# Diffusion over pairs of tiles, with its first sums kept on chip and the output stage in the same block

## The chip, the cores and the metric

The kernel runs as one program on one core of a Trainium2 chip, all in float32. The metric is the device time of one execution in microseconds (us); lower is better. Three timed runs of the kernel before gave 3935.77, 3936.57 and 3945.05 us, so the median is 3936.57 us. Five engines work side by side, each on its own list of instructions: TensorE (PE: matmuls, with the weight loads as PEld), VectorE (DVE), ScalarE (ACT), GpSimd (POOL, which also issues the indirect transfers) and SyncE (SP, which issues most plain transfers). They wait for each other on semaphores.

## The reference

Four graph layers stand behind each other, each followed by x = layernorm(x + layer(x)). There are 50,000 nodes with 256 features and 12,500 edges, sorted by destination. The first two layers are attention over edges, the third is an edge MLP, and the fourth is the diffusion that the change is about:

```
def _spmm(h, src, dst, inv_deg):
    agg = jax.ops.segment_sum(h[src], dst, num_segments=h.shape[0])
    return agg * inv_deg[:, None]

# layer 3: edge MLP and gate
core = relu(concat(x[src], edge_attr) @ W1 + b1) @ W2 + b2
msg  = sigmoid(concat(x[src], edge_attr) @ Wg + bg) * core
x    = layernorm(layernorm(segment_sum(msg, dst) + x) * gamma + beta + x)

# layer 4: diffusion, six steps
x = silu(h @ W_in.T + b_in)
out = term = x
for i in range(1, 7):
    term = _spmm(term, src, dst, inv_deg) / i
    out = out + term
x = out @ W_out.T + b_out
result = layernorm(h + x)
```

Only nodes that are the destination of an edge get anything from the sums. For all other nodes the four layers are plain row by row arithmetic. The kernel computes all 50,000 rows in that plain way, and afterwards writes the rows of the destination nodes over them.

## The kernel before

**Tables.** The edges lie in T = 100 tiles of 128 slots. For each tile a 128x128 matrix in `eq_tab` says which slots share a destination; a matmul with it sums the messages of each destination. The diffusion works on a table `h` in memory. Its first R = 12,800 rows belong to the tiles; the next R rows (silu of source nodes that are no destination) never change. `table_row` says for each edge which row of the table to gather. A destination can begin in one tile and go on in the next, so after each step the first two rows of every tile are read back (`load_ends`), one matmul with `upper` carries sums across tiles, and the result (`B`, 100 rows) is scattered into the table (`put_bound`). Only then may the next step gather.

**The edge MLP** (`mlp`) runs over 50 pairs of tiles. Its last operation is the silu on ACT into a buffer `HH`, which SP stores to `h`.

**The diffusion** (`diffuse`, L2688) does six steps, by Horner's rule: new row = sum of gathered rows * inv_deg/(6-s) + h. At the start ACT issues ten transfers that bring the 100 tiles of `h` into the on-chip buffer `acc` (L2814) and four that copy the second half of `h` to a second table `h2` (L2818), because the steps read one table and write the other. For every tile and step there is one gather (POOL, L616), one load of the equality matrix (SP, L2726), one matmul (PE, `total`, L2801), one combined multiply and add (DVE, `add`, L2838) and one store (SP, L2731).

**Dense units beside it.** In the same block the class `Dense` computes 160 units of 256 plain rows each. Its instructions are written out in turns: one turn per unit, 165 turns with filling and draining. In a turn PE does four groups, `project` (L810), `transpose` (L674), `out_project` (L828) and `hidden` (L819), and between the groups there are four gaps. `places` (L2676) gives every tile of the diffusion a gap: 110 gaps to a step, a tile in nearly each of the first 100, and the tile-crossing sum five gaps before the end. PE does a tile's sum in its gap, DVE its add one gap later, SP its store two gaps later; POOL gathers eight tiles ahead. POOL also computes all powers of a turn in one instruction (`powers`, L926), for three units in different phases. This power feeds ACT's scales (L851) and DVE's third norm (L900); those feed, one turn later, the variance that the next power needs.

**The output stage** (`output`, L2860 on) is a block of its own behind a barrier. For 50 pairs it loads the sums and `x3`, transposes, multiplies by `w_out`, adds, squares, takes one power per two pairs on POOL (L2894) and writes each tile to `out` by an indirect transfer that POOL issues (L2900).

**What sets the order.** Nothing is scheduled by a tool: each engine follows its own list, written by the loops over turns and gaps, and waits on semaphores. A wait holds up everything behind it on its engine.

## Time and profile before

| what | before |
|---|---|
| median of three timed runs | 3936.57 us |
| span of the profiled execution | 3924.5 us |
| between that span and the median | 12.1 us |
| PE / PEld / DVE / ACT / POOL busy | 83% / 67% / 72% / 48% / 53% |
| edge MLP | about 1800 to 2397 us of the span |
| diffusion block, first instruction to last | 2406.6 to 3723.4 us |
| output block, first instruction to last | 3732.4 to 3914.2 us |

The span runs from the first to the last event of one execution that the profiler recorded. Shares of busy time are means over all stages. What a change does in a stage is read from that stage: which instruction there waits, for what, and whether a later one waits in its turn.

### The profile page before, as it was taken

The numbers are of one execution on the slowest core, as the hardware profiler recorded it, in microseconds if no ns is written. First come the engines' busy times: TensorE is split into PE (matmuls) and PEld (weight loads), VectorE is DVE, ScalarE is ACT, GpSimd is POOL, SyncE is SP. The second block draws the span as 40 slices with busy tenths as digits, with TensorE's granted clock in tenths as the row PEclk, the third lists the DMA queues.
The fourth block names the chain that finished last, engine by engine and source line by source line (L and its number), as shares of the span: only waits on it lengthen the run. The fifth ranks groups of instructions, "written<-read, shape, count | busy, mean of one in ns | idle before, by whom it ended". The sixth has DMA issues, their size and how long they took to land. (4 is left out here: it accounts for less than half of the span.)

```text
span 3924.5 us, 56642 instructions
## 1 busy us (share of the span) xinstructions
PE 3261.1 (83%) x14868; PEld 2626.7 (67%) x14868; DVE 2815.4 (72%) x7890; ACT 1882.4 (48%) x5403; POOL 2087.1 (53%) x2120
## 2 busy tenths in 40 slices
PE   5999927688576899477999993599999999999865
PEld 4888715476454566245777772587878787888754
DVE  5676768698587466794666662598989898989733
ACT  3777705466333121142333331366666666666555
POOL 4767500475365666033333322476767676767667
PEclk8999958899799999657999996799999999999998
DMA  5788739443375333183333335886868686878765
GB/s 145 244 244 247 235 95 354 153 134 108 107 211 174 94 88 87 54 247 99 111 116 115 111 110 187 283 252 199 251 201 252 197 251 201 253 208 242 209 210 164
DMA packets 690467, 710.71 MB, mean 181 GB/s; under 512 B 73444, under 2 KB 644190, under 8 KB 689796
## 3 DMA queue, kind: packets, MB, share of 16 engines
q1 hardware_dynamic: 592204, 484.13, 39.8%
q0 software_dynamic: 68288, 181.26, 17.1%
q10 hardware_dynamic: 29660, 41.70, 3.2%
q8 instruction: 126, 2.06, 0.2%
q14 instruction: 189, 1.55, 0.1%
HBM read 427.77 MB, written 296.22 MB: 184 GB/s over the span
## 5 line engine op out<-in xcount | busy, mean ns | idle before, releaser
L616 POOL DMA_INDIRECT s_i_messages<-h,table_row x600 | 614.0, 1023 | 190.4 <-issue 158.3
L2801 PE MATMUL s_i_bank<-s_i_messages,s_i_equal 128*128 128x256 f32 x1200 | 362.5, 386 | 74.3 <-issue 36.6
L926 POOL TENSOR_TENSOR n_powers<-n_powers,neg_half 128x8 f32<-128x8 f32 (+3 forms) x164 | 268.5, 1637 | 229.9 <-DVE n_powers L891 149.4
L851 ACT ACTIVATE n_z<-gamma_bc,n_powers 128x256 f32<-128x256 f32 x320 | 174.8, 593 | 356.5 <-POOL n_powers L926 356.5
L810 PE MATMUL s_n_bank<-w,n_xt 128*128 128x256 f32 x1280 | 306.9, 383 | 22.6 <-DMA n_xt<-in_x_t 22.6
L828 PE MATMUL s_n_bank<-w_out,n_ht 128*128 128x256 f32 x1280 | 311.7, 387 | 5.6 <-ACT n_ht L838 5.3
L2838 DVE SCALAR_TENSOR_TENSOR s_i_y<-s_i_bank,s_i_scale,s_i_acc 128x256 f32<-128x256 f32 x600 | 285.2, 476 | 34.3 <-PE s_i_bank L2801 32.2
L819 PE MATMUL s_n_bank<-n_x3t,w_in 128*128 128x256 f32 x1280 | 303.2, 380 | 0.0
L2801 PEld LDWEIGHTS s_i_bank<-s_i_messages,s_i_equal 128*128 128x128 f32 x1200 | 219.3, 193 | 101.1 <-issue 42.2
L810 PEld LDWEIGHTS s_n_bank<-w,n_xt 128*128 128x128 f32 x1280 | 246.0, 192 | 58.0 <-DMA n_xt<-in_x_t 23.8
L828 PEld LDWEIGHTS s_n_bank<-w_out,n_ht 128*128 128x128 f32 x1280 | 247.3, 195 | 46.2 <-ACT n_ht L838 11.9
L819 PEld LDWEIGHTS s_n_bank<-n_x3t,w_in 128*128 128x128 f32 x1280 | 243.9, 191 | 33.4
L616 POOL DMA_INDIRECT s_a_x<-in_x,index x200 | 197.8, 989 | 97.4 <-issue 96.3
L2101 PE MATMUL s_e_ps_qv<-w_qv,s_e_xt 128*128 128x512 f32 x400 | 189.7, 597 | 0.0
L2116 ACT ACTIVATE s_e_xt<-s_e_ps_t 128x512 f32<-128x512 f32 x100 | 59.7, 597 | 264.3 <-PE s_e_ps_t L2091 264.3
L2405 POOL TENSOR_TENSOR s_g_small<-s_g_small,neg_half 128x2 f32<-128x2 f32 (+1 forms) x51 | 43.7, 857 | 243.2 <-DVE s_g_small L2648 243.2
L2640 DVE SCALAR_TENSOR_TENSOR s_g_y<-s_g_x,real,s_g_bank 128x512 f32<-128x512 f32 x50 | 37.3, 747 | 179.5 <-PE s_g_bank L2496 179.5
L682 ACT ACTIVATE n_squares<-n_u 128x256 f32<-128x256 f32 x320 | 130.2, 408 | 73.2 <-issue 62.5
L2536 ACT ACTIVATE s_g_h<-s_g_hidden,real 128x512 f32<-128x512 f32 x50 | 36.1, 722 | 251.0 <-DVE s_g_hidden L2595 175.8
L900 DVE TENSOR_SCALAR n_x<-n_z,n_small,n_powers 128x256 f32<-128x256 f32 x320 | 118.3, 412 | 50.9 <-POOL n_powers L926 37.2
L695 ACT ACTIVATE n_x3t<-s_n_bank 128x512 f32<-128x512 f32 x160 | 95.4, 596 | 108.6 <-PE s_n_bank L674 103.9
L859 ACT ACTIVATE n_w<-n_w,n_powers 128x256 f32<-128x256 f32 x320 | 142.8, 493 | 9.1 <-POOL n_powers L926 9.1
(444 smaller groups left out, 9169.7 us busy)
## 6 DMA issues: line engine op xcount, KB each, us to landing
h<-s_i_y SPq DMA_DIRECT2D x600, 128.0 KB, 3.9
n_xt<-in_x_t SPq DMA_DIRECT2D x160, 256.0 KB
out<-n_w SPq DMA_DIRECT2D x160, 256.0 KB
s_i_equal<-eq_tab SPq DMA_DIRECT2D x600, 64.0 KB
x<-s_x_rows SPq DMA_DIRECT2D x100, 256.0 KB
out<-s_a_hs SPq DMA_DIRECT2D x100, 128.0 KB
proj_dst<-s_a_hd SPq DMA_DIRECT2D x100, 128.0 KB
h<-s_h_rows SPq DMA_DIRECT2D x50, 256.0 KB, 4.1
```

The source lines that it names most:

```text
L616: return net.nc.gpsimd.indirect_dma_start(out, None, table, bass.IndirectOffsetOnAxis(index, 0))
L682: sq = self.nc.scalar.activation(self.squares[0][:, g, :], self.U[u][:, g, :], ACT.Square, scale=self.D ** -0.5, accum_out=self.S[u][:, g: ...
L810: mm = self.nc.tensor.matmul(self.pr[:, g * self.D:(g + 1) * self.D], self.XT[u][:, c, g * P:(g + 1) * P], self.net.w12[:, c, :], start=c ...
L819: mm = self.nc.tensor.matmul(self.hd[:, 2 * m * P:2 * (m + 1) * P], self.net.w_in[:, c, m * P:(m + 1) * P], self.X3T[:, c, :], start=c == ...
L828: mm = self.nc.tensor.matmul(self.op[:, g * self.D:(g + 1) * self.D], self.HT[:, m, g * P:(g + 1) * P], self.net.w_out[:, m, :], start=m = ...
L851: sc = self.nc.scalar.activation(self.Z[u][:, g, :], self.net.bc["gamma"][:], ACT.Identity, bias=v[:, 8 + g:9 + g], scale=v[:, 10 + g:11 + g])
L859: nm = self.nc.scalar.activation(self.W[u][:, g, :], self.W[u][:, g, :], ACT.Copy, scale=v[:, 14 + g:15 + g])
L900: nm = self.nc.vector.tensor_scalar(self.X3[u][:, g, :], self.Z[u][:, g, :], s[:, 24 + 2 * g:25 + 2 * g], v[:, 12 + g:13 + g], ALU.subtrac ...
L926: self.nc.gpsimd.tensor_tensor(v[:, 8 + b0:8 + b1], v[:, b0:b1], self.net.neg_half[:, 0:b1 - b0], ALU.pow).then_inc(self.powered, 1)
L2101: mm = nc.tensor.matmul(qvs[b][:, :], XT[b][:, c, :], net.w_qv[:, c, :], start=c == 0, stop=c == C - 1)
L2801: nc.tensor.matmul(banks[r % 4][:, 0:D], EQ[q % NM][:], M[q % NM][:], start=True, stop=True).then_inc(summed, 1)
L2838: V.scalar_tensor_tensor(Y[q % NY][:], banks[r % 4][:, 0:D], scale[:, s, t:t + 1], acc[:, t, :], ALU.mult, ALU.add).then_inc(added, 1)
```

## The change

- **Pairs.** `diffuse` handles two tiles per place: one load of two equality matrices, two gathers, two matmuls into one bank, one DVE instruction over 512 columns, one store. Buffers hold six pairs of messages and five pairs of results; gathers run four pairs ahead.
- **First sums on chip.** `mlp` writes its silu directly into `net.acc`, a buffer that lives on into the diffusion, and SP stores `h` from there. Only row 1 of every tile is read back at the start of the diffusion.
- **No table copy.** One table of 3R rows takes the place of the two. Even steps read rows 0 to 2R, odd steps rows R to 3R, with a second set of row numbers (`table_row_odd`, `bound_row_odd`). A few small instructions in `setup` and in the search compute these.
- **Equality matrices scaled ahead.** `mlp` multiplies each matrix by inv_deg after its use (two ACT instructions per pair) and stores it back to `eq_tab`; the diffusion's add then has a constant factor.
- **Wider borders.** `places` now lays 50 pairs over 96 gaps and leaves 15 gaps free before the next step. The crossing sum, its add and the scatter follow the last pair by 7, 8 and 9 gaps; the ends are loaded 5 gaps behind it.
- **Last step** leaves its result in `acc` and stores nothing. Twelve extra gaps follow the last turn.
- **Output in the same block.** The transposes read `acc`. The result overwrites `acc` and is normed and written from there. One power serves four pairs. The crossing rows go through the same steps apart (`XB`, `YB`) and are written last, after all other writes have landed.

```diff
-        self.h = dram("h", [2 * R, D])
-        self.h2 = dram("h2", [2 * R, D])
+        self.h = dram("h", [3 * R, D])
...
+            def store_eq(k):
+                if 0 <= k < N:
+                    sp.wait_ge(eq_scaled, k + 1)
+                    sp.dma_start(net.eq_tab[k * G:(k + 1) * G, :, :].rearrange("g p e -> p g e"), EQ[k % NE][:]).then_inc(eq_out[k % NE], 16)
...
+                    out, real = (net.acc[:, k * G:(k + 1) * G, :], net.real) if k < N else (HE[:], net.ones)
+                    nc.scalar.activation(out, HB[0:p, 0:w, :], ACT.Silu, scale=real[0:p, 0:1]).then_inc(h_ready, 1)
+            def scale_eq(k):
+                if 0 <= k < N:
+                    act.wait_ge(summed, k + 1)
+                    for g in range(G):
+                        t = k * G + g
+                        sc = nc.scalar.activation(EQ[k % NE][:, g, :], EQ[k % NE][:, g, :], ACT.Copy, scale=net.inv_deg[:, t:t + 1])
+                    sc.then_inc(eq_scaled, 1)
...
+def places(U, gaps, hold):
+    span = (gaps - (STEPS - 1) * hold - 4) // STEPS
+    at, last = {}, []
+    for s in range(STEPS):
+        g0 = s * (span + hold)
+        for k in range(U):
+            at[g0 + k * span // U] = (s, k)
+        last.append(g0 + (U - 1) * span // U)
...
+        ends_at = {g + 5: s for s, g in enumerate(last)}
+        total_at = {g + 7: s for s, g in enumerate(last)}
+        bound_at = {g + 8: s for s, g in enumerate(last)}
+        put_at = {g + 9: s for s, g in enumerate(last[:-1])}
...
+                else:
+                    sp.wait_ge(added, nth(s, U - 1))
+                    sp.dma_start(net.ends.rearrange("t r d -> r t d"), net.acc[0:2, :, :]).then_inc(ends_out, 16)
+                    sp.wait_ge(ends_out, 16)
+                    sp.dma_start(EF[:], net.ends[:, :, :]).then_inc(ends_in, 16)
...
+                rows, tab = (net.table_row_odd, net.h) if s % 2 else (net.table_row, net.h[0:2 * R, :])
+                for g in range(G):
+                    t = k * G + g
+                    gather(net, M[q % NM][:, g, :], tab, rows[:, t:t + 1]).then_inc(got[q % NM], 16)
...
+            for u in range(2):
+                gp.wait_ge(dn.stored[u], 16 * (dn.units // 2))
+            for i in range(LATE):
+                if i % Q == 2:
+                    power((i - 6) // Q)
+                write(i - 8)
+            gp.wait_ge(written, 16 * T)
+            gp.wait_ge(o_ready, U + 1)
+            nc.gpsimd.indirect_dma_start(a["out"], bass.IndirectOffsetOnAxis(net.bound_out[:, 0:1], 0), YB[:], None,
+                                         bounds_check=N - 1, oob_is_err=False).then_inc(written, 16)
...
-            for c in range(T // CHUNK):
-                act.dma_start(acc[:, c * CHUNK:(c + 1) * CHUNK, :],
-                              net.h[c * CHUNK * P:(c + 1) * CHUNK * P, :].rearrange("(t p) d -> p t d", p=P)).then_inc(acc_in[c], 16)
-            for c in range(4):
-                rows = slice(R + c * (R // 4), R + (c + 1) * (R // 4))
-                act.dma_start(net.h2[rows, :], net.h[rows, :]).then_inc(copied, 16)
+            act.dma_start(net.acc[1:2, :, :], net.h[0:R, :].rearrange("(t p) d -> p t d", p=P)[1:2, :, :]).then_inc(first_in, 16)
...
-                    V.scalar_tensor_tensor(Y[q % NY][:], banks[r % 4][:, 0:D], scale[:, s, t:t + 1], acc[:, t, :], ALU.mult, ALU.add).then_inc(added, 1)
+                    out = Y[q % NY][:] if s < STEPS - 1 else pair(k)
+                    V.scalar_tensor_tensor(flat(out), banks[r % 4][:, :], 1.0 / (STEPS - s), flat(pair(k)), ALU.mult, ALU.add).then_inc(added, 1)
...
-def output(net, tab):
```

The first place is the border between the second and third step on POOL. `s_i_messages` is what a gather fills, `n_powers` the Dense units' powers, `s_i_bound` the crossing rows. Before:

```order
1011 L616 DMA s_i_messages<-h,table_row 128x256
1012 L926 TENSOR_TENSOR n_powers<-n_powers,neg_half 128x8 x3
1013 L2769 DMA h<-s_i_bound,bound_row 25600x256
1014 L616 DMA s_i_messages<-h,table_row 128x256 x4
1015 L926 TENSOR_TENSOR n_powers<-n_powers,neg_half 128x8
1016 L616 DMA s_i_messages<-h,table_row 128x256 x5
1017 L926 TENSOR_TENSOR n_powers<-n_powers,neg_half 128x8
```

And now:

```order
1011 L625 DMA s_i_messages<-h,table_row_odd 128x256 x2
1012 L935 TENSOR_TENSOR n_powers<-n_powers,neg_half 128x8 x4
1013 L2848 DMA h<-s_i_bound,bound_row 38400x256
1014 L625 DMA s_i_messages<-h,table_row 128x256 x8
1015 L935 TENSOR_TENSOR n_powers<-n_powers,neg_half 128x8 x2
1016 L625 DMA s_i_messages<-h,table_row 128x256 x4
1017 L935 TENSOR_TENSOR n_powers<-n_powers,neg_half 128x8
```

At this border eight gathers, where there were four, now stand between the scatter and the next power. Over the five borders the gathers there were 8, 4, 8, 4 and 8 before, and are 6, 8, 2, 4 and 6 now.

The second place is POOL's way from the diffusion into the output. Before:

```order
1217 L926 TENSOR_TENSOR n_powers<-n_powers,neg_half 128x2 x2
1218 L2769 DMA h<-s_i_bound,bound_row 25600x256
1219 L926 TENSOR_TENSOR n_powers<-n_powers,neg_half 128x2
1220 L47 UNCONDITIONAL_BRANCH
1221 L49 ISA
1222 L2888 UNCONDITIONAL_BRANCH
1223 L2894 TENSOR_TENSOR s_j_small<-s_j_small,neg_half 128x4
1224 L2900 DMA out<-s_j_y,end_node 50000x256 x2
1225 L2894 TENSOR_TENSOR s_j_small<-s_j_small,neg_half 128x4
1226 L2900 DMA out<-s_j_y,end_node 50000x256 x4
```

And now:

```order
1211 L935 TENSOR_TENSOR n_powers<-n_powers,neg_half 128x2 x3
1212 L2871 TENSOR_TENSOR s_j_small<-s_j_small,neg_half 128x8
1213 L2877 DMA out<-h_acc,end_node 50000x256 x4
1214 L2871 TENSOR_TENSOR s_j_small<-s_j_small,neg_half 128x8
1215 L2877 DMA out<-h_acc,end_node 50000x256 x8
```

The last scatter and the barrier between the two are gone, and a power of eight columns stands ahead of every eight writes where one of four columns stood ahead of every four.

The third place is POOL's start of the diffusion, now:

```order
916 L2879 MEMSET s_j_x_bound 100x256
917 L2881 DMA s_j_x_bound<-x,bound_row 100x256
918 L625 DMA s_i_messages<-h,table_row 128x256 x12
919 L935 TENSOR_TENSOR n_powers<-n_powers,neg_half 128x4
920 L625 DMA s_i_messages<-h,table_row 128x256 x6
```

Two instructions for the crossing rows of the output and twelve gathers come before the first power.

## Rows read from the trace of the kernel before

**Rows 1.** Windows: stretch, its length, busy us (instructions) per engine, PEclk, DMA, GB/s.

```profile
2000.00:2100.00 100.00, 100.00 (x466) 79.09 (x466) 64.50 (x180) 37.77 (x72) 33.42 (x45) 1.00 0.37 111
2406.00:2520.00 114.00, 37.59 (x134) 29.78 (x135) 26.93 (x75) 12.76 (x40) 34.08 (x33) 0.62 0.98 315
2520.00:2640.00 120.00, 120.00 (x589) 105.71 (x588) 113.87 (x314) 78.63 (x245) 93.38 (x81) 1.00 0.85 246
2655.00:2715.00 60.00, 50.66 (x238) 42.90 (x238) 45.53 (x126) 34.14 (x106) 32.29 (x29) 0.97 0.57 167
```

**Rows 2.** Timeline of PE, one turn: start us, busy us, engine, line, operation.

```profile
3001.45 1.89 PE L810 MATMUL s_n_bank<-w,n_xt 128*128 128x256 f32 x8
3003.18 0.59 PE L2801 MATMUL s_i_bank<-s_i_messages,s_i_equal 128*128 128x256 f32 x2
3003.61 0.60 PE L674 MATMUL s_n_bank<-ident,n_x 128*128 128x128 f32 x4
3004.05 0.60 PE L2801 MATMUL s_i_bank<-s_i_messages,s_i_equal 128*128 128x256 f32 x2
...
3008.80 0.38 PE L810 MATMUL s_n_bank<-w,n_xt 128*128 128x256 f32 x1
```

**Rows 3.** Timeline of POOL, the same turn; in brackets its idle time before.

```profile
2999.68 1.66 POOL L926 TENSOR_TENSOR n_powers<-n_powers,neg_half 128x8 f32<-128x8 f32 x1 [0.27 <-DVE n_powers L891]
3001.54 1.15 POOL L616 DMA_INDIRECT s_i_messages<-h,table_row  x1 [0.19 <-issue]
...
3005.61 0.95 POOL L616 DMA_INDIRECT s_i_messages<-h,table_row  x1 [0.31 <-issue]
3006.87 1.67 POOL L926 TENSOR_TENSOR n_powers<-n_powers,neg_half 128x8 f32<-128x8 f32 x1 [0.32 <-DVE n_powers L891]
```

**Rows 4.** Timeline, start of the diffusion on ACT and ACT's DMA queue (ACTq).

```profile
2406.61 40.78 ACTq L2814 DMA_DIRECT2D s_i_acc<-h  x10
...
2447.43 5.63 ACTq L2818 DMA_DIRECT2D h<-h  x4
2453.10 0.42 ACT L682 ACTIVATE n_squares<-n_u 128x256 f32<-128x256 f32 x1 [62.46 <-issue]
```

**Rows 5.** Timeline of all engines at the first border, SP's queue among them (SPq).

```profile
2671.11 0.31 SPq L2736 DMA_DIRECT2D s_i_ends<-h  x1
...
2673.99 1.64 POOL L926 TENSOR_TENSOR n_powers<-n_powers,neg_half 128x8 f32<-128x8 f32 x1 [4.80 <-DVE n_powers L891]
...
2674.45 0.65 PE L2797 MATMUL s_i_bank<-s_i_ends,upper 100*100 100x256 f32 x2 [3.36 <-DMA s_i_ends<-h]
...
2676.48 1.07 POOL L2769 DMA_INDIRECT h<-s_i_bound,bound_row  x1 [0.85 <-DVE s_i_bound L2832]
...
2680.45 1.00 POOL L616 DMA_INDIRECT s_i_messages<-h,table_row  x1 [2.90 <-DMA h<-s_i_bound,bound_row]
...
2690.44 1.67 POOL L926 TENSOR_TENSOR n_powers<-n_powers,neg_half 128x8 f32<-128x8 f32 x1
...
2693.00 0.66 PE L674 MATMUL s_n_bank<-ident,n_x 128*128 128x128 f32 x4 [4.29 <-DVE n_x L900]
```

**Rows 6.** Timeline, end of the diffusion and start of the output.

```profile
3716.21 0.69 DVE L875 TENSOR_TENSOR n_w<-n_w,b_out_bc 128x512 f32<-128x512 f32 x1
...
3722.45 0.91 ACT L859 ACTIVATE n_w<-n_w,n_powers 128x256 f32<-128x256 f32 x2 [4.61 <-POOL n_powers L926]
...
3736.32 0.60 ACT L2938 ACTIVATE s_j_xt<-s_j_ps_t 128x512 f32<-128x512 f32 x1 [12.96 <-PE s_j_ps_t L2917]
```

**Rows 7.** Source L2900: min/median/max ns, first and last start us.

```profile
L2900 POOL DMA_INDIRECT out<-s_j_y,end_node x100: 967/981/1417, 3750.4 to 3913.2; - x100
...
DMA to landing us min/median/max: 2.0/3.8/4.3
```

**Rows 8.** Source L2894, the same columns.

```profile
L2894 POOL TENSOR_TENSOR s_j_small<-s_j_small,neg_half x25: 1049/1247/1386, 3747.2 to 3905.5; 128x4 f32<-128x4 f32 x25
```

**Rows 9.** DMA issues of the page: count, KB each, median us to landing.

```profile
h<-s_i_y SPq DMA_DIRECT2D x600, 128.0 KB, 3.9
...
h<-s_h_rows SPq DMA_DIRECT2D x50, 256.0 KB, 4.1
```

485 lines of the change are left out of this document (262 added, 223 removed).

## The prediction, written before the changed kernel ran

> **What bounds the kernel now.** I read the windows first. In the edge MLP PE is busy for all of 100 us, ACT for 38 of them [rows 1]. In the body of the diffusion PE is again busy for 120 of 120 us at the full clock, DVE for 114, POOL for 93, and the DMA engines for 0.85 of the time. There 589 PE instructions take 120 us, 0.204 us each. Two other stretches fall short of that. From 2406 to 2520 us, the start of the diffusion, there are 134 instructions, 27.3 us of work in 113.4 us (the block starts at 2406.6): 86 us are lost. From 2655 to 2715 us, the first border between two steps, there are 238, 48.5 us of work in 60: 11.5 us are lost.
>
> The timeline of PE then gives the price of a turn [rows 2]. `project` holds PE for 1.73 us (3001.45 to 3003.18), a tile's sum for 0.43, the transposes for 0.43 to 0.44, and the whole turn with four tiles lasts 7.35 us. A Dense unit thus costs PE 3 x 1.73 + 0.43 = 5.62 us, and the block's PE work is 160 x 5.62 + 600 x 0.43 = 1157 us. It lasts 1317 us, so some 160 us are the start, the borders and the drain.
>
> POOL is close behind [rows 3]: power to power takes 7.19 us, of which it waits 0.32, so its own work is 6.87 us for a power and four gathers. Where the tiles pause, the powers come 4.80 + 1.64 = 6.44 us apart [rows 5]: this is the loop from power over ACT's scales and DVE back to the power, 0.82 us longer than PE's 5.62.
>
> The start is explained by ACT [rows 4]: its queue takes 40.8 us to issue the ten loads of `acc` and 5.6 us more for the copies, and its first computing instruction comes at 2453.1, after 62 us of idleness. All Dense units need it. At the end, the output stage is POOL's: 100 writes from 3750.4 to 3913.2 us [rows 7].
>
> **The change part by part.**
>
> *Pairs.* PE's work stays: two sums of 0.43 us each. They stand together, and rows 2 show no loss between groups that a pair could save. DVE's add has 512 columns instead of twice 256, and one fixed part less; DVE doesn't bound. A turn of the body now carries 4.17 tiles (50 pairs in 96 gaps), so PE needs 5.62 + 4.17 x 0.43 = 7.41 us and POOL 6.87 + 0.17 x 1.26 = 7.08 us. PE stays the bound and the total of its work is the same: 0. If pairing freed something, DVE being late somewhere, it would show as less than 7.41, which PE's rows exclude; a loss is rival A.
>
> *Start.* The ten loads and the copies go, the load of one row per tile remains. What is late next is POOL: two instructions for the crossing rows (about 2.2 us, estimated from a gather of 1.26 us and something short of a power), twelve gathers of 0.95 + 0.31 = 1.26 us [rows 3], 15.1 us, and only then the first power, at about 2424. A power comes 5.4 us after the start of its turn (3001.45 to 3006.87), so turn 1 starts in effect at 2418.6. The 134 instructions are reached after 5.6 turns (three of 16, one of 28, then 36 a turn). Hence 4.6 x 7.35 = 33.8 us later, at 2452.4, the new kernel stands where the old one stood at 2520: 67.6 us gained. Bounds: PE alone would need 27.3 us after some 5 us of loading, which gives 80; if gathers and loads stay slow together, half, 40. I take 68, since it rests on rows.
>
> *Borders.* At the first border POOL issues the scatter 2.5 us after a power, takes 1.07 us, waits 2.90 us for it to land, and issues eight gathers before the next power: 16.45 us from power to power instead of 6.44, so 10.0 us late [rows 5]. DVE and then PE wait for that power (PE 4.29 us at 2693.0). With the 2.5 free turns at 0.82 us the sum is 12.0, and 11.5 were measured. Now 6, 8, 2 + 6, 4 + 4 and 6 gathers stand there. The same sum gives 2.5 + 1.07 + 2.90 + 6 x 1.26 - 6.44 = 7.6 us for six, 10.1 for eight, and I take 9 and 8.5 for the two cases in which a power comes between: 8.6 on average. The free stretch has grown to four turns, 3.3 us. Together 11.9 - 0.5 = 11.4 us, against 11.5. So the wider border gives 0: it removes the wait of the first pairs, but POOL's scatter, wait and gathers still stand ahead of a power, and behind the power wait ACT, DVE and PE. PE's wait for the ends (3.36 us) stays too: SP issues their load behind the store of a Dense unit's rows. Bounds: 3.3 us per border if all of POOL's delay is absorbed (gain 41), 17 if none is and the second delay adds (loss 28).
>
> *End of the diffusion.* Before, the last Dense unit's sum is ready at 3716.9 and the output's first ACT instruction comes at 3736.3, 19.4 us later [rows 6]. Now ACT must still finish the last norm (3723.4, 6.5 us), and PE must wait for the ends that SP stores and reads back, and transpose: I add 1.1 us, 7.6 in all. Gain 11.8.
>
> *First write.* From that ACT instruction to the first write 14.1 us pass, for a power of two pairs. The power of four pairs needs two more, each 1.73 + 0.43 us on PE [rows 2]: 4.3 us lost (up to 6.6, at the old write rate).
>
> *Writes.* 99 intervals last 162.8 us [rows 7]. A write takes 0.98 + 0.30 us, 126.7 in all; 36.1 us are left for 24 powers, 1.50 each, of which 1.25 is the power itself [rows 8]. Now twelve powers of eight columns stand between the writes, 1.66 us each [rows 3] and 0.25 around: 22.9 us. Gain 13.2; nothing if ACT can't follow.
>
> *Last row.* The crossing rows wait until all writes have landed, 3.8 us [rows 7], and cost one more issue, 1.3: 5.1 lost.
>
> *Edge MLP and setup.* Two more ACT instructions per pair lie beside a PE that has no gap and an ACT that is idle for 62 of 100 us: 0. One more store per pair meets DMA engines busy for 0.37. Some seven small DVE instructions in the setup: 1 us lost.
>
> Sum: 67.6 + 0 + 11.8 - 4.3 + 13.2 - 5.1 - 1 = 82 us. The profiled execution's span is 3924.5 us, so the new span is 3842; with the 12.1 us between span and median this gives 3854 us.
>
> **The rivals.**
>
> A. POOL becomes the bound of the body. Its margin is 7.41 - 7.08 = 0.33 us a turn, and two turns of 24 hold six gathers. For it: the first gather after a power takes 1.15 us, not 0.95. If the rest drifted halfway to that, with their share of waits, a turn would be 7.6 us: 144 turns x 0.19 = 27 us, time 3881. Against it: the turn of rows 3 already contains the slow gather. The Trainium skill ("SBUF — State Buffer", SBUF: two separate sides) says that a DMA issued from GpSimd is held up in writing its descriptors while VectorE runs an instruction in a two-port mode. The rows show at most a fifth of a microsecond of this; by that rule with every gather at 1.15 us the turn would be 7.9 us and the time about 3925.
>
> B. The borders cost the full 17 us: 3882. C. The borders shrink to 3.3 us because the loop had slack: 3813.
>
> D. Slower than before. The transfers in pairs take longer, the DMA engines become the bound. They are busy 0.85 of 7.35 us now, 6.2 us a turn, and 6.4 with 4.17 tiles. The change turns slower when a body turn reaches 7.41 + 82/144 = 7.98 us, a quarter more than 6.4. If the stores and matrix loads together took 2 us more per turn, 8.4 us, the time would be 3854 + 144 x 1.0 = 3997. Against it: the pieces per partition stay as long, and 256 KB land in 4.1 us where 128 KB take 3.9 [rows 9]. The Trainium skill ("SBUF — State Buffer", A bandwidth-pool intuition that's wrong) gives about 358 GB/s between memory and one core; the start, at 315 GB/s and a DMA share of 0.98, agrees, and 246 in the body leaves room.
>
> E. The change doesn't do what it says in the MLP: the scaling of the matrices delays `tanh` and then PE by all of its time, about 0.66 us on 50 pairs: 33 us, 3887. Against it stands ACT's idleness.
>
> **How the numbers follow.** Chances: forecast 0.59, A 0.10, B 0.12, C 0.10, D 0.04, E 0.05. What can be told from no change is about 0.3%, 12 us. All cases but D are faster by more than that; between D and the others I leave 0.01 for no change: 0.95, 0.01, 0.04. The range reaches to C below and a little beyond B and E above, 3816 to 3890. It takes in half the bounds of the start and of the borders, and leaves out D, both ends of the borders, and A by its rule.
>
> **What would show it.** Right: first computing ACT instruction within 20 us of the block's start; steady turns of 7.4 us with PE at 100%; border windows of 60 us short of 55 to 60 instructions; first write some 18 us after the first transposed pair is moved; 100 writes in 150 us. Wrong: POOL without waits before its powers in the body and PE waiting for messages (A); a DMA share near 1 (D); MLP turns longer than before (E); border windows short by fewer than 30 instructions (C) or by more than 80 (B).

## The result

The change made the kernel faster, by half of what was forecast.

| | before | after | forecast |
|---|---|---|---|
| median of four timed runs, us | 3938.15 | 3896.88 | 3854 |
| range of the runs, us | 3935.77 to 3945.05 | 3894.42 to 3901.2 | 3816 to 3890 |
| ratio of the times (95% interval) | 1 | 0.9896 (0.9882 to 0.9910) | 0.979 |
| span of the profiled execution, us | 3924.5 | 3892.7 | 3842 |

The profiled execution of after has a hole ahead of the diffusion, in the projection of queries, keys and values (PE waits 7.67 us there at 1311.9 us), that before has not, and its diffusion block starts at 2416.3 instead of 2406.6 us. From the block's start to the end of the span before took 1517.9 us and after 1476.4, 41.5 us less. The timed runs gained 41.3 us.

So it is the profiled execution of before that is unusual. Its span is 12.1 us below the median of the timed runs, where every other execution on record has a span about 1.8 us below its time; no timed execution of before has a span under 3928.5 us, and this one has 3924.5. All 16 traces of the changed kernel and its edits that can be read show the hole (PE waits 6 to 8 us there). The timed executions of before very likely have it too, but none of them was traced, and what the hole is stays open. The forecast of the time doesn't suffer, as its gain of 82 us can be taken from the median as well; a span of 3842 us was too low by some 10 us from the outset. All times below are taken from the start of the block.

One execution is left out of all times and readings: the profiled one of the run with both parts of the start put back took 9747.6 us, its 256-column matmuls 836 ns each on average at a granted clock of 1.00, and what disturbed it stays open.

| stretch, us from the block's start | before | after | gain | forecast |
|---|---|---|---|---|
| last sum of the last Dense unit | 1310.3 | 1272.0 | 38.3 | 67.6 |
| from there to ScalarE's first output instruction | 19.4 | 15.3 | 4.1 | 11.8 |
| from there to the first write | 14.1 | 19.0 | -4.9 | -4.3 |
| first write to last write | 162.8 | 154.6 | 8.2 | 13.2 |
| last write to the end | 11.3 | 15.6 | -4.3 | -5.1 |

The windows of after, in the columns of [rows 1]: the edge MLP, the first 100 us of the diffusion, and the stretch around the second border.

```profile
2010.00:2110.00 100.00, 100.00 (x467) 79.09 (x466) 64.56 (x180) 43.26 (x90) 33.36 (x45) 1.00 0.40 123
2416.00:2516.00 100.00, 82.64 (x369) 68.76 (x370) 66.14 (x171) 42.53 (x133) 75.60 (x69) 0.92 0.76 220
...
2840.00:2860.00 20.00, 9.95 (x46) 7.96 (x44) 8.52 (x22) 7.42 (x22) 11.79 (x11) 0.81 0.28 81
2860.00:2880.00 20.00, 19.92 (x82) 17.00 (x83) 15.20 (x41) 11.70 (x39) 10.77 (x9) 0.85 0.54 157
```

The MLP did not change: 467 PE instructions per 100 us against 466, though ScalarE has 43 us of work instead of 38. The start is as forecast: GpSimd's first power comes 17.5 us after the block's start (forecast 17.4), and PE has issued its 134th instruction of the block after 48.9 us instead of 113.4, 64.5 us earlier (forecast 67.6). So about 26 us of the start's gain were lost again before the end of the diffusion. PE's waits from 100 us after the block's start to the last Dense sum (1172.0 us), with their number and the longest:

```profile
PE s_n_bank L837 <- ACT n_ht L847: 21.0, 27, 1.2
PE s_n_bank L683 <- DVE n_x L909: 20.7, 7, 9.2
PE s_i_bank L2909 <- DMA s_i_ends<-h: 15.7, 5, 4.5
```

And in before, between the same two points (1210.3 us; L837 is its L828, L683 its L674, L2909 its L2797):

```profile
PE s_n_bank L674 <- DVE n_x L900: 19.5, 5, 4.5
PE s_i_bank L2797 <- DMA s_i_ends<-h: 13.6, 5, 3.4
PE s_n_bank L828 <- ACT n_ht L838: 5.3, 8, 1.0
PE s_i_bank L2801 <- DMA s_i_messages<-h,table_row: 4.2, 3, 1.5
```

The sum went from 42.6 to 57.4 us. What is new are the short waits for the hidden layer's activation, 27 instead of 8. Eight of the 27, 7.8 us, stand in the bodies of the steps, each behind six gathers between two powers; most of the others stand at the borders. The waits for `n_x` stand at the borders, but for 0.5 to 1 us. They hardly grew in sum but are spread otherwise: in order of the borders 4.3, 3.8, 3.3, 3.7 and 4.5 us before, and 2.5, 9.2, 3.4, 3.3 and 1.5 now. GpSimd's timeline shows where one comes from (start us, busy us, in brackets the idle time before). It corresponds to [rows 3]:

```profile
3002.40 1.07 POOL L625 DMA_INDIRECT s_i_messages<-h,table_row  x1 [0.18 <-issue]
...
3008.11 0.96 POOL L625 DMA_INDIRECT s_i_messages<-h,table_row  x1 [0.30 <-issue]
...
3009.37 0.96 POOL L625 DMA_INDIRECT s_i_messages<-h,table_row  x1 [0.30 <-DVE n_powers L900]
...
3010.35 1.67 POOL L935 TENSOR_TENSOR n_powers<-n_powers,neg_half 128x8 f32<-128x8 f32 x1
...
3012.05 1.09 ACT L860 ACTIVATE n_z<-gamma_bc,n_powers 128x256 f32<-128x256 f32 x2 [3.43 <-POOL n_powers L935]
...
3014.72 1.99 PE L837 MATMUL s_n_bank<-w_out,n_ht 128*128 128x256 f32 x8 [0.97 <-ACT n_ht L847]
```

Six gathers stand between two powers here. The power's inputs are ready at 3009.12, and it starts at 3010.35. ScalarE waits for the power with its scales, its norm and, behind them, the activation `n_ht`; PE waits 0.97 us for that. At the second border the scatter and eight gathers stand between two powers, the second power comes 16.5 us behind the first, and PE's wait is the longest of the five borders:

```profile
2858.20 1.12 PE L683 MATMUL s_n_bank<-ident,n_x 128*128 128x128 f32 x4 [9.21 <-DVE n_x L909]
...
2860.08 3.78 PE L837 MATMUL s_n_bank<-w_out,n_ht 128*128 128x256 f32 x8 [0.76 <-ACT n_ht L847]
```

Behind the wait eight matmuls take 3.78 us, where they take 1.99 after the short one: the clock has fallen from 2.4 to 1.2 GHz for them (in the 20 us from 2860 the granted clock is 0.85). Over the whole stretch the granted clock is 0.98 (before 0.99).

The balance closes if both kernels are compared over the same work. From its 134th instruction to the last Dense sum PE issues 5558 instructions in both. Before, this takes 1196.9 us: 1152.5 busy and 42.6 of waits. Now it takes 1223.1 us: 1162.3 busy and 59.2 of waits. So the loss of 26.2 us is 16.6 us of waits and 9.8 us of slower instructions, and most of the slow ones are at the lower clock.

At the end of the diffusion (compare [rows 6]; SPq is SyncE's queue):

```profile
3687.59 0.69 DVE L884 TENSOR_TENSOR n_w<-n_w,b_out_bc 128x512 f32<-128x512 f32 x1
3688.04 0.33 SPq L2804 DMA_DIRECT2D ends<-h_acc  x1
...
3698.25 0.31 SPq L2806 DMA_DIRECT2D s_i_ends<-ends  x1
...
3701.53 1.14 PE L2909 MATMUL s_i_bank<-s_i_ends,upper 100*100 100x256 f32 x2 [14.70 <-DMA s_i_ends<-ends]
...
3703.56 0.60 ACT L2972 ACTIVATE s_j_xt<-s_n_bank 128x512 f32<-128x512 f32 x1 [12.32 <-PE s_n_bank L2940]
```

SyncE stores the last ends at 3688.04 and can load them back only 10.2 us later. PE waits 14.70 us for them in front of its first transposes; the prediction gave this wait 1.1 us.

The writes and their powers (minimum, median and maximum ns; first and last start), for [rows 7] and [rows 8]:

```profile
L2877 POOL DMA_INDIRECT out<-h_acc,end_node x100: 974/976/1532, 3722.5 to 3877.1; - x100
```

```profile
L2871 POOL TENSOR_TENSOR s_j_small<-s_j_small,neg_half x13: 1055/1698/2042, 3718.8 to 3866.8; 128x8 f32<-128x8 f32 x12, 128x4 f32<-128x4 f32 x1
its engine sat idle before it (us, times) until:
  DVE s_j_small L3058: 31.6, 3
```

The powers cost what was forecast (1.70, forecast 1.66). But among the writes GpSimd waits some 5 us: 3.1 in two waits for DVE's variance (31.6 less the first, 28.5) and 1.8 for ScalarE's norms.

**A measure for the steps.** The add of the crossing rows (L3012, before L2832) stands once at each border. Its first and fifth lie four steps apart: before at 2675.1 and 3514.4, 209.8 us a step; after at 2619.7 and 3486.3, 216.7 us. PE's own work, by the prediction's prices, is 27.5 turns x 5.62 + 43 = 197.6 us before and, with 111 gaps to a step, 27.75 x 5.62 + 43 = 199.0 after. So a step lost 12.2 us before and 17.7 after, body and border together. The prediction had the same loss for both. The experiments below are read by this period too.

### The profile page after: what moved, and what is told of

Its sections match the earlier page's. It is cut to its first block and busy times, and to the rows that moved or that the text cites. A ratio compares the mean times of both kernels' runs of the same rounds, so it can differ in the third digit from the quotient of the medians.

```text
span 3892.7 us, 54725 instructions
## 1 busy us (share of the span) xinstructions
PE 3260.4 (84%) x14874; PEld 2617.8 (67%) x14874; DVE 2757.0 (71%) x7581; ACT 1912.7 (49%) x5507; POOL 2091.8 (54%) x2111
## 3 DMA queue, kind: packets, MB, share of 16 engines
q0 software_dynamic: 68352, 181.28, 16.6%
## 5 line engine op out<-in xcount | busy, mean ns | idle before, releaser
L625 POOL DMA_INDIRECT s_i_messages<-h,table_row_odd x300 | 313.8, 1046 | 91.4 <-issue 83.5
L625 POOL DMA_INDIRECT s_i_messages<-h,table_row x300 | 311.9, 1040 | 89.6 <-issue 81.8
L837 PE MATMUL s_n_bank<-w_out,n_ht 128*128 128x256 f32 x1280 | 317.5, 392 | 22.2 <-ACT n_ht L847 22.2
L2914 PE MATMUL s_i_bank<-s_i_messages,s_i_equal 128*128 128x256 f32 x1200 | 309.4, 381 | 2.8 <-issue 2.0
L828 PE MATMUL s_n_bank<-n_x3t,w_in 128*128 128x256 f32 x1280 | 305.4, 382 | 0.0
L837 PEld LDWEIGHTS s_n_bank<-w_out,n_ht 128*128 128x128 f32 x1280 | 242.0, 195 | 63.3 <-ACT n_ht L847 30.4
L828 PEld LDWEIGHTS s_n_bank<-n_x3t,w_in 128*128 128x128 f32 x1280 | 246.1, 192 | 34.9 <-issue 0.2
L3019 DVE SCALAR_TENSOR_TENSOR s_i_y<-s_i_bank,h_acc 128x512 f32<-128x512 f32 x250 | 170.4, 682 | 6.9 <-PE s_i_bank L2914 3.5
L2557 ACT ACTIVATE h_acc<-s_g_hidden,real 128x512 f32<-128x512 f32 x50 | 36.1, 723 | 233.0 <-DVE s_g_hidden L2625 169.8
```

The lines of the kernel that those rows point to most:

```text
L625: return net.nc.gpsimd.indirect_dma_start(out, None, table, bass.IndirectOffsetOnAxis(index, 0))
L828: mm = self.nc.tensor.matmul(self.hd[:, 2 * m * P:2 * (m + 1) * P], self.net.w_in[:, c, m * P:(m + 1) * P], self.X3T[:, c, :], start=c == ...
L837: mm = self.nc.tensor.matmul(self.op[:, g * self.D:(g + 1) * self.D], self.HT[:, m, g * P:(g + 1) * P], self.net.w_out[:, m, :], start=m = ...
L2914: mm = nc.tensor.matmul(banks[r % 4][:, g * D:(g + 1) * D], EQ[q % NM][:, g, :], M[q % NM][:, g, :], start=True, stop=True)
L3019: V.scalar_tensor_tensor(flat(out), banks[r % 4][:, :], 1.0 / (STEPS - s), flat(pair(k)), ALU.mult, ALU.add).then_inc(added, 1)
```

## The experiments

Each is one edit of the changed kernel, timed in one of four groups beside the kernel before (3935.8 to 3938.7 us in the four). The changed kernel was timed once more in the first group as a control, and all differences below are from its 3895.4 us. Read by the ratios they come out up to 3.5 us otherwise. HOLD is the number of free gaps ahead of the next step.

> The changed kernel itself, unedited, as the measure for the other three on the same chip. All theories: ratio to before 0.988 to 0.991. In its profile, the hole of some 10 us in the projection of queries, keys and values (1300 to 1315 us) is expected to be absent, if it is an event of that one execution.

Measured: 3895.4 us, ratio 0.9891 (0.9875 to 0.9906), period 216.3. The hole ahead of the diffusion is there again (6.73 us of waiting), so it was not an event of one execution.

| edit | us | ratio (95% interval) | period of a step, us |
|---|---|---|---|
| none (control) | 3895.4 | 0.9891 (0.9875 to 0.9906) | 216.3 |
| gathers paced in bodies | 3890.0 | 0.9882 (0.9866 to 0.9898) | 215.4 |
| gathers paced everywhere | 4000.6 | 1.0159 (1.0143 to 1.0175) | not read |
| HOLD 11 | 3872.1 | 0.9835 (0.9821 to 0.9848) | 212.5 |
| crossing sum, add and scatter two gaps later | 3877.1 | 0.9853 (0.9838 to 0.9868) | 213.2 |
| no crossing rows | 3860.9 | 0.9798 (0.9785 to 0.9812) | none to read |
| last ends in pieces | 3891.2 | 0.9890 (0.9871 to 0.9908) | 216.2 |
| and last crossing sum late | 3886.6 | 0.9868 (0.9853 to 0.9883) | 216.4 |
| loads of the start put back | 3909.9 | 0.9936 (0.9923 to 0.9950) | 215.6 |
| copies of the start put back | 3930.7 | 0.9977 (0.9968 to 0.9986) | 217.1 |
| both put back | 3963.4 | 1.0063 (1.0050 to 1.0077) | not read |
| no scaling in the MLP | 3898.4 | 0.9905 (0.9891 to 0.9919) | 215.9 |
| power per two pairs | 3895.4 | 0.9900 (0.9885 to 0.9914) | 215.8 |
| HOLD 11, last sum late ("b") | 3862.1 | 0.9798 (0.9784 to 0.9812) | 212.0 |
| b, crossing sum, add and scatter two gaps later | 3864.0 | 0.9812 (0.9795 to 0.9829) | 211.5 |
| b, crossing sum two gaps later, add and scatter one | 3861.5 | 0.9810 (0.9797 to 0.9822) | 211.1 |

**GpSimd's order in the body.**

```diff
-                    upto_q = min((s + 1) * U, s * U + k + AHEAD + 1)
-                if fetched < upto_q:
+                    upto_q = min((s + 1) * U, s * U + k + AHEAD + 3)
+                border = any(g <= i < g + 12 for g in put_at)
+                if fetched < upto_q and (border or i < 8 or i % 2 == 0):
```

> Against the changed kernel (ratio to before 0.9896, 3897 us). The edit: in the body of a step GpSimd issues its gathers in every second gap only, so never more than two pairs (four gathers) between two powers; borders as they are, PE's order untouched. Theory (GpSimd's order): the trace after shows PE waiting about 1 us for the hidden layer's activation, behind a late power, once in every turn that follows six gathers; nine such turns lie in the bodies. They vanish: 9 to 12 us faster, ratio about 0.987, and the waits of PE at out_project fall from 27 (21 us) by nine or more. Rival 1 (the turn with three pairs is long on PE or ScalarE for its own reasons, since PE still does three pairs there): within 3 us of the changed kernel. Rival 2 (fewer gathers in hand starve PE): slower, with PE waits for messages.

The edit also lets the gathers run two pairs further ahead. Measured 3890.0 us, 5.4 below the control: less than expected, and its interval overlaps the control's. PE's waits at `out_project` did fall from 27 (22.5 us) to 16 (12.6 us), and all eight in the bodies behind six-gather turns are gone. So the theory of where they come from holds. But waits for messages (4.4 us, all in the first step) and a longer wait for `n_x` (25.6 us instead of 22.5) came instead; over the four steps the period fell by 0.9 us.

The same without the exception for borders:

> The edit: as the one before, and in the borders too: after the scatter at most four gathers per turn, 2, 4, 0, 2 and 2 before the next power instead of 6, 8, 2 (then 6), 4 (then 4) and 6. Theory (the gathers issued in a lump behind the scatter delay the power): the power behind the scatter comes 2.5 + 1.07 + 2.9 + 2 x 1.26 - 6.44 = 2.6 us late instead of 7.6 to 10.1; five borders gain 3 to 5 us each, 15 to 25 in all, on top of the 9 to 12 of the bodies: 3862 to 3873 us, ratio 0.981 to 0.984; PE's waits for n_x at the borders fall from 20.7 us to under 8. Rival (the border is set by the round trip of the ends and of the scatter, and by the free turns, not by the lump): no more than 5 us below the run with paced bodies alone.

Measured 4000.6 us, 105 above the control, where 22 to 33 below was expected. The first half of the theory is right: PE's wait for `n_x` falls from 22.5 to 4.8 us. But PE now waits for messages in 53 places, 99 us in all:

```profile
PE s_i_bank L2915 <- DMA s_i_messages<-h,table_row: 71.1, 33, 5.9
PE s_i_bank L2915 <- DMA s_i_messages<-h,table_row_odd: 28.2, 20, 2.5
```

Two pairs to a turn are less than the 50/24 = 2.08 that PE takes. The gathers in one go behind the scatter were what restored GpSimd's lead in every step. Spread out, it starts a step with less, and the waits say that the lead is used up before the step's end.

**HOLD 11 instead of 15**: 50 pairs in 100 gaps, none with six gathers to a turn in the bodies, four free gaps less.

```diff
-    G, NM, NY, AHEAD, HOLD, EXTRA = 2, 6, 5, 4, 15, 12
+    G, NM, NY, AHEAD, HOLD, EXTRA = 2, 6, 5, 4, 11, 12
```

> The edit: HOLD 11 instead of 15, so that 50 pairs lie in exactly 100 gaps, one in every second gap, and a step has four free gaps less at its end (POOL's order shows at most four gathers per turn in the bodies, no turn with six, and 8, 8, 8, 6 or 6 around the scatters). In the run with paced bodies ten waits at out_project went (22.5 to 12.6 us), but 4 us of waits for messages came, since there GpSimd's lead shrank by two pairs in every step. Here the lead stays. Theory (each six-gather turn costs about 1.1 us, the free turns 0.8 us each): 10 us for the bodies and 5 x 0.8 = 4 us for the turns, less some 1 to 3 us per border in which the first pair now waits for its messages (four gaps behind the scatter instead of eight): between 3880 and 3895 us, PE's waits at out_project at 12 to 14 us, and new waits for messages only at the borders. Rival (free gaps behind the scatter are what hides the gathers): slower than 3900 us.

Measured 3872.1 us, 23 below the control and beyond the expected range. PE's waits, for the stretch behind the first 100 us:

```profile
PE s_i_bank L2909 <- DMA s_i_ends<-h: 16.0, 5, 4.3
PE s_n_bank L683 <- DVE n_x L909: 9.5, 8, 2.2
PE s_n_bank L837 <- ACT n_ht L847: 8.0, 14, 1.2
PE s_i_bank L2914 <- DMA s_i_messages<-h,table_row: 3.0, 1, 3.0
```

Against the paced run the wait for `n_x` fell from 24.3 to 9.5 us in this stretch. That was not expected, and the timeline of the first border shows the reason:

```profile
2640.05 1.03 PE L2914 MATMUL s_i_bank<-s_i_messages,s_i_equal 128*128 128x256 f32 x4
...
2641.42 1.67 POOL L935 TENSOR_TENSOR n_powers<-n_powers,neg_half 128x8 f32<-128x8 f32 x1
...
2643.97 0.66 PE L683 MATMUL s_n_bank<-ident,n_x 128*128 128x128 f32 x4 [1.17 <-DVE n_x L909]
```

The next step's first pair now stands ahead of the transposes that wait for the late power, so PE has work in the hole; in the control no pair stands there, and PE waits 2.43 us. At the second border the power still comes 15.2 us behind the one before it (16.5 in the control), but PE's waits for `n_x` there fall from 8.9 to 1.2 us, with 3.0 us for the first pair's messages. In the kernel before three tiles stood in that place at the first border, and PE waited 4.29 us all the same. The edit changes four things at once (free turns, six-gather turns, the gathers around the scatters, the place of the first pair), and no run told their shares apart.

**Where the crossing sum stands.**

```diff
-        total_at = {g + 7: s for s, g in enumerate(last)}
-        bound_at = {g + 8: s for s, g in enumerate(last)}
-        put_at = {g + 9: s for s, g in enumerate(last[:-1])}
+        total_at = {g + 9: s for s, g in enumerate(last)}
+        bound_at = {g + 10: s for s, g in enumerate(last)}
+        put_at = {g + 11: s for s, g in enumerate(last[:-1])}
```

> The edit: the crossing sum, its add and the scatter come 9, 10 and 11 gaps behind the last pair instead of 7, 8 and 9; the load of the ends stays at 5. In the changed kernel PE waits 3.1 us for the ends at each border (15.3 us in five). Theory (PE's wait for the ends is lost Dense time on the path): PE's waits for the ends fall below 5 us in all and the time by 8 to 12 us, to 3884 to 3888 us. Rival (in the free turns the loop from power to power, 6.44 us, sets the pace, and the wait for the ends hides in it): within 3 us of 3896; or slower, as the scatter and the gathers then come closer to the next step.

Measured 3877.1 us, 18 below. The waits for the ends went from 15.3 us to 1.2, the wait for `n_x` rose from 22.5 to 28.4: the theory's mechanism, and more than its size. In the traces the diffusion, from the block's start to the last Dense sum, is 13.2 us shorter (1259.1 against 1272.3); the rest lies ahead of it (2.9) and in the writes (3.9), which the edit doesn't touch.

```diff
-        ends_at = {g + 5: s for s, g in enumerate(last)}
+        ends_at = {last[L] + 5: L}
...
-                gp.wait_ge(added, nth(s, U))
-                nc.gpsimd.indirect_dma_start(net.h, ..., B[:], None, ...)
+                for b in range(NY):
+                    gp.wait_ge(stored[b], 16 * (U // NY) * (s + 1))
```

> Leaves out, in the first five steps, the crossing rows: the load of the ends, their sum and its add, and the scatter. GpSimd waits for the last stores of the step instead. Everything else stays, the free gaps too. Theory (a border costs some 13 us in the changed kernel: 3.3 us of free turns, the wait for the ends, and a power that comes late by scatter, landing and gathers): power behind the border is late by about 0.5 + 6 to 8 x 1.26 + 1.66 - 6.44, 3 to 5 us, instead of 7.6 to 10; five borders gain 5 x (3.1 + 4) = 35 us at most, 20 at least: 3861 to 3876 us. Rival (the lump of gathers alone delays the power, and the round trips are hidden beside it): less than 10 us.

Measured 3860.9 us, 34.5 below the control, at the upper end of the theory: the crossing rows cost 7 us a border in the changed kernel. The wait for `n_x` fell from 22.5 to 13.7 us.

**The end of the diffusion.**

```diff
-                    sp.dma_start(net.ends.rearrange("t r d -> r t d"), net.acc[0:2, :, :])...
-                    sp.wait_ge(ends_out, 16)
+            def store_last_ends(n):
+                sp.wait_ge(added, nth(STEPS - 1, (n + 1) * (U // 5) - 1))
+                tl = slice(n * (T // 5), (n + 1) * (T // 5))
+                sp.dma_start(net.ends[tl, :, :].rearrange("t r d -> r t d"), net.acc[0:2, tl, :])...
```

> The edit: in the last step the two end rows of each tile are stored in five pieces of 20 tiles as soon as they are summed, instead of in one transfer of 100 tiles after the last sum. In the changed kernel that transfer takes 10.2 us (3688.04 to 3698.25), and PE waits 14.70 us. Theory (the transfer itself is slow, all its 200 rows lie in two partitions): the last piece takes about 2 to 4 us, PE's wait falls to 6 to 8 us, the time by 6 to 9 us. Rival (it stands in the queue behind the Dense units' stores and loads): the last piece takes as long as the whole one, time unchanged within 2 us.

The last piece:

```profile
3687.66 0.33 SPq L2800 DMA_DIRECT2D ends<-h_acc  x1
...
3690.92 0.32 SPq L2810 DMA_DIRECT2D s_i_ends<-ends  x1
...
3694.16 1.15 PE L2915 MATMUL s_i_bank<-s_i_ends,upper 100*100 100x256 f32 x2 [7.70 <-DMA s_i_ends<-ends]
```

A fifth of the data, 40 KB, takes 3.3 us instead of 10.2, with the same stores ahead of it in the queue. So the transfer itself is slow: 160 KB more cost 6.9 us, which is 23 GB/s. The Trainium skill ("DMA: Bandwidth & Descriptors", Why a DMA increments its semaphore by 16 and not by 1) says that the number of DMA engines that share a transfer is the largest one up to 16 that divides the slowest dimension of both sides; here that is the two partitions, so two engines. Two of the 16 would have 39 of the 315 GB/s that the kernel before reached at the start of its diffusion [rows 1], an estimate; the slope is of that order but lower. No run here changed the shape of the transfer or shows which DMA engines took part. PE's wait fell from 14.7 to 7.7 us as expected, but timed, the edit gave 4.2 us instead of 6 to 9, and the intervals overlap.

Then the crossing sum as well, behind the tenth pair of the output, and x loaded ahead of the read-back:

```diff
             for i in range(U + 2):
+                if i == 10:
+                    total(STEPS - 1, U)
                 transposes(i)
```

> The edit: the ends of the last step are stored in five pieces as in the run before; SyncE loads the first four pairs of x before it waits for them and reads them back; PE's last crossing sum stands behind the tenth pair of the output, DVE's add with it. Theory (the wait on PE stands wholly on the path of the output): PE's wait of 14.6 us becomes one of under 5 us, first write 10 us earlier, time 3884 to 3889 us against 3895.4 (storing in pieces alone gave 3891.2). Rival (the last Dense rows, or x, are what the first output pair really waits for): no better than 3891.

Measured 3886.6 us, 8.8 below the control. From the start of the last Dense sum to the first write it takes 23.4 us instead of 34.7.

```profile
3690.43 1.06 PE L2950 MATMUL s_n_bank<-ident,h_acc 128*128 128x128 f32 x8 [0.98 <-DVE n_w L882]
...
3690.66 0.33 SPq L2800 DMA_DIRECT2D ends<-h_acc  x1
```

PE transposes the first pair before the ends are even stored.

**The start.** Ten loads of `acc` put back, then the four copies, then both:

```diff
+            for c in range(10):
+                act.dma_start(net.acc[:, c * 10:(c + 1) * 10, :], net.h[...]).then_inc(first_in[c], 16)
+            for c in range(4):
+                rows = slice(R + c * (R // 4), R + (c + 1) * (R // 4))
+                act.dma_start(net.h2[rows, :], net.h[rows, :]).then_inc(copied, 16)
```

> Puts back one part of the kernel before: at the start of the diffusion ScalarE issues ten transfers that load all of the table's first half into the on-chip buffer (1.28 MB each), though it is there already, and the adds of the first step wait for them; no table copy. Theory (ScalarE's queue holds it for 40.8 us, and the Dense units with it): the first computing ScalarE instruction comes about 42 us after the block's start instead of 9.8, and the time is 30 to 50 us above the changed kernel, 3926 to 3946 us. Rival (the gain at the start came from the copies, 4 x 3.3 MB, that no longer fill the DMA engines): less than 15 us above.

> Puts back the other part of the start of the kernel before: four transfers on ScalarE's queue that copy the second half of the table (13 MB) to a second table, which nothing reads here; the ten loads stay out. Putting back the ten loads alone gave 3909.9 us, 14.5 above the changed kernel (3895.4). Theory (the rest of the 64 us gained at the start is traffic: the copies fill the DMA engines behind the loads, so that gathers, matrices and columns of the Dense units come late): 25 to 45 us above the changed kernel, 3920 to 3940 us, with a DMA share above 0.9 in the first 60 to 80 us of the block. Rival (loads and copies only cost ScalarE's issue time, 5.6 us for the copies): less than 8 us above.

> Puts back both parts of the start of the kernel before, ten loads and then four copies on ScalarE's queue (the second table is read by nothing). Alone the loads cost 14.5 us (3909.9) and the copies 35 (3930.7). Theory (they compound: behind the loads the copies still fill the DMA engines when the Dense units start, as in the kernel before): 55 to 68 us above the changed kernel, 3950 to 3963 us, so that without its new start the changed kernel would be slower than the one before. Rival (they share the same hole): no more than 40 above, 3935.

Measured: loads alone +14.5 us, though ScalarE's first computing instruction comes 40.5 us after the block's start. Copies alone +35.3, though their issue takes 2.5 us:

```profile
2419.40 2.53 ACTq L2968 DMA_DIRECT2D h<-h  x4
...
2465.47 2.08 PE L2917 MATMUL s_i_bank<-s_i_messages,s_i_equal 128*128 128x256 f32 x4 [38.02 <-DMA s_i_equal<-eq_tab]
```

PE waits 38 us for small loads of the equality matrices, which SyncE issued, beside copies that ScalarE issued: its first sum comes 47 us after the block's start, against 10 in the changed kernel. The Trainium skill ("DMA: Bandwidth & Descriptors", Issuing engines are not separate DMA queues) says that all queues end on the same 16 DMA engines and interleave; the row agrees that they share. It also shows how much a small load can lose: in the 40 us from the block's start the DMA engines were busy all the time at 330 GB/s, and 13.1 MB at that rate take 40 us. So the load waited for nearly the whole of the copies. Both together: +68.0, which is 18 more than the two alone, so they compound. How they do was not seen, as this run has no usable trace. The forecast's term for the start (67.6) is confirmed, though ScalarE's issue time, by which it was explained, is only a part of it. The run also shows that without the new start the change would be slower than before by 0.5 to 0.8%.

**MLP and output.**

```diff
-                scale_eq(i - 2)
```

> Leaves out the scaling of the equality matrices by inv_deg in the edge MLP and their store back (100 ScalarE instructions, 50 stores), so that the diffusion adds unscaled sums; the ring of six matrix buffers stays. Theory (ScalarE is idle for more than half of the MLP, and PE has no gap there): within 3 us of 3895. Rival E of the prediction (the scaling delays tanh and then PE): 20 to 33 us faster.

Measured 3898.4 us: the intervals overlap, and it is no faster than the control. Rival E is out.

```diff
-        NB, Q = 4, 4
+        NB, Q = 4, 2
```

> The output stage takes one power per two pairs again (25 of four columns) instead of one per four pairs (12 of eight and one of four). Forecast by the prediction's own terms: the first write comes 4.3 us earlier, and the writes take 13.2 us longer; in the changed kernel they took 154.6 us instead of the forecast 149.6. Theory (the power of four pairs brought 8 us in the writes and cost 4.9 at the first write): 3 us slower, 3897 to 3900 us, writes 161 to 163 us. Rival (writes are limited by ScalarE's norms or by landing, not by powers): writes under 157 us and the time 2 to 5 us below 3895.

Measured 3895.4 us, equal. The writes take 156.6 us against 154.6: the longer power brings 2 us, not 13, and even that is not clear of the scatter (in the other traces with this output stage unedited they take 150.8 to 154.7 us). The first write comes 16.8 us after ScalarE's first output instruction instead of 19.0, so the longer power costs 2.2 us there, not 4.3. Most of the 8.2 us gained on the writes must come from the rest of the new stage (no loads of the sums, other distances between the stages); which part was not tried.

**Together.** b has HOLD 11 and the late last sum. In the next run the crossing sum, its add and the scatter come two gaps later. In the last run the edit is not what its expected text says: PE's sum stands at 9 gaps as in the run before it, and only the add (9) and the scatter (10) are one gap later than in b.

> HOLD 11 (100 gaps to a step; 3872.1 us alone) together with the edit of end_late. Theory (separate places, so the gains add; in the run with HOLD 11 the wait for the last ends had grown to 18.4 us): 10 to 14 us below 3872, 3858 to 3862 us. Rival (as before): 3868 or above.

> As best_b, and the crossing sum, its add and the scatter two gaps later (9, 10, 11 behind the last pair; alone 3877.1, 18 below the changed kernel). Two gaps are then left between the scatter and the first pair of the next step. Theory 1 (PE's wait for the ends, 16.0 us in five borders with HOLD 11, is time on the path): 8 to 14 us below best_b, 3846 to 3853 us. Theory 2, the rival (both edits fill the same hole, and the first pair now waits for its gathers, which issue 2.5 + 1.3 us and land some 3 us behind the scatter's landing): within 5 us of best_b, PE's waits for messages taking the place of those for the ends.

> Between best_b (crossing sum 7 gaps behind the last pair, 3862.1 us, 15.3 us of waits for ends and 4.3 for messages) and best_a (9 gaps, 3864.0 us, no wait for ends and 28 us for messages): 8, 9 and 10 gaps. Theory (two costs with an optimum between): waits for ends about 7 us and for messages under 12 in five borders, 3 to 6 us below best_b, 3856 to 3859 us. Rival (the chain from the last store over the ends, the scatter and the first gather sets the border, wherever PE waits for it): within 2 us of 3862.

b measured 3862.1 us: the two gains add (23.3 + 8.8 = 32.1 of 33.3). The later crossing sums, worth 18 us alone, now bring nothing. PE's waits in b:

```profile
PE s_i_bank L2919 <- DMA s_i_ends<-h: 15.3, 5, 4.3
PE s_n_bank L683 <- DVE n_x L909: 13.4, 7, 3.3
```

and in the last run:

```profile
PE s_i_bank L2924 <- DMA s_i_messages<-h,table_row_odd: 13.9, 3, 5.6
...
PE s_i_bank L2924 <- DMA s_i_messages<-h,table_row: 7.3, 2, 3.7
PE s_n_bank L683 <- DVE n_x L909: 3.1, 5, 1.2
PE s_i_bank L2919 <- DMA s_i_ends<-h: 1.1, 1, 1.1
```

The waits for the ends have become waits for messages (28.0 us of them in the run with two gaps). The three times lie within 2.5 us of each other, which fits the rival: with few free gaps left, the chain from the last store over ends, scatter and gathers to the first pair sets the border, wherever PE waits in it. A sum at 8 gaps was not tried. b and the last run, 3862 us, beat both kernels: 1.9 to 2.0% under before, 0.9% under the changed one.

## Why the prediction was wrong

- **Start**, 67.6: right in size (64.5 in the trace, 68.0 timed), and the new limit, GpSimd's first power, came when forecast. What the old start cost was explained by the 40.8 us in which ScalarE issues loads [rows 4]; alone the loads cost 14.5 us, and the copies, whose issue is short, 35.3.
- **Body**, 0: wrong. "PE stays the bound" holds for the mean of a turn, 7.08 against 7.41 us. But the two turns in 24 with six gathers were averaged into it. GpSimd's work in such a turn is 6.87 + 2 x 1.26 = 9.4 us, while PE's, with six sums, is 5.62 + 6 x 0.43 = 8.2. So the power comes 1.2 us late, and PE waits for it at once. The order of the instructions showed these turns; a price for each could have been worked out. They cost 1.0 us of waiting each; taking them out brought 5 us, within the uncertainty.
- **Borders**, 0 (11.4 against 11.5): wrong, and the largest miss. A step loses 17.7 us instead of 12.2; of these 5.5 us the waits in the bodies are 1.6. The prediction priced a border as 8.6 us for the late power and 3.3 for the free turns, less the 0.5 by which the same sum missed the border before (12.0 against 11.5); it counted the wider stretch as relief for the first pairs. It took the late power's delay as a constant of GpSimd's order. But PE's wait is that delay less the work that PE finds meanwhile, and a later first pair is work taken out of the wait. HOLD 11 fits this: 23 us, of which by its own theory at most 10 are the six-gather turns and 4 the free turns. It is argued and not shown in full, since the kernel before had this work in the wait and yet waited longer for `n_x` at four of the five borders. The traces do show what grew: one wait of 9.2 us at the second border (3.8 before), the short waits for the hidden layer, and the instructions at the lower clock. How the remaining 9 us of HOLD 11 divide stays open. The prediction also took PE's wait for the ends for settled ("stays too"). It stayed (13.6 and 15.7 us), and removing it brought 18 us in this kernel, none in b.
- **End of the diffusion**, 11.8: the mechanism was named, its size was not looked at. 1.1 us for storing and reading back the ends and transposing stood against 14.7 us of waiting, 10.2 of them for the store; the term came out at 4.1. The lag of such a transfer had no row, and no bound was given for it.
- **First write** -4.3 (measured -4.9): right in size, in part by luck, as the longer power explains 2.2 of it (power per two pairs). **Last row** -5.1 (-4.3): right.
- **Writes**, 13.2: measured 8.2, and the part of the powers in it is at most 2. The mechanism was wrong: the gain comes from somewhere else in the stage.
- **MLP and setup**: the MLP's 0 is right.
- **Rivals**: A named the right engine and the turns with six gathers, but looked for the wrong sign (PE waiting for messages), and its turns of 7.6 us throughout did not come. B (borders at 17 us) is the nearest, its time of 3882 too low only because the end and the writes fell short as well. C, D and E are out.

Sum of the misses: start -3, steps -26, end -8, first write -1, writes -5, last row +1, setup about +1: 82 becomes 41.

## What to carry to other kernels

Where an engine in order carries the pulse of a loop (here one power per turn), don't average its load: list what stands between two pulses, and hold each list against the work of the slowest engine in that same turn. A free stretch at a border is not only slack; work moved out of it may be work that no longer fills a wait. A wait that is removed may only move along its chain: two edits that each gave 18 and 23 us gave 23 together.

## What the runs showed of the hardware

- A transfer of 200 rows of 1 KB from two partitions took 10.2 us, 40 rows 3.3 us. In the changed kernel the load of the same rows at the borders, from memory into 100 partitions, kept PE waiting for 4.5 us at most.
- Beside four copies of 3.3 MB, whose issue took 2.5 us, PE waited 38 us for 128 KB loads of another queue.
- Behind a wait of 9.2 us PE's next eight matmuls of 256 columns took 3.78 us instead of 1.99, with a granted clock of 0.85 in those 20 us.
